# Row gathers in pairs and held-back scatters in layer 0 of a two-layer graph network, on one core

## The reference

```python
h = maximum(layernorm(x), 0)
msg = relu(h[src] + edge_attr_16 @ W_edge.T + b_edge)          # layer 0
agg = segment_sum(msg, dst, 6250)
x = x + (relu(batchnorm((h + agg) @ W1.T + b1)) @ W2.T + b2)
h = maximum(layernorm(x), 0)
Y = relu(concat(h[src], edge_attr_64) @ M_W.T + M_b)           # layer 1
Z = segment_sum(Y, dst, 6250)
x = x + relu(concat(h, Z) @ U_W.T + U_b)
```

## Time and profile before

| | us |
|---|---|
| Median of three runs (lowest, highest) | 4233.39 (4220.89, 4243.19) |
| Profiled execution, own time | 4231.45 |
| Span of the profiled execution | 4229.6 |
| Turns 2 to 29 of layer 0, those that the change touches | about 415 to 2947 of the span |
| Layer 1, paced turns and rest | about 3260 to 4180 of the span |
| Busy over the span: PE / PEld / DVE / ACT / POOL | 2624.5 / 2201.3 / 1525.2 / 965.0 / 2087.3 |

### The profile page before, as it was taken

One profiled execution on the slowest core, in us unless ns is written; L12 is line 12 of the kernel. 1 busy time (PEld: TensorE's weight loads), 2 busy tenths in 40 slices (PEclk: granted clock), 3 DMA queues, 4 the chain that ended last, 5 costly groups with the idle time before them and its releaser, 6 DMA issues.

```text
span 4229.6 us, 74366 instructions
## 1 busy us (share of the span) xinstructions
PE 2624.5 (62%) x25733; PEld 2201.3 (52%) x25733; DVE 1525.2 (36%) x2605; ACT 965.0 (23%) x2153; POOL 2087.3 (49%) x2185
## 2 busy tenths in 40 slices
PE   3456666566566556666656665656465767676665
PEld 3345555455455455555545555555454655555554
DVE  4323233223223323222323222323234555555553
ACT  1322222122222222222222222222134222222221
POOL 5444545544545544545454545544523455555554
PEclk9767666666666666667666667666676788878786
DMA  7545544545444544544454544544334666666661
GB/s 223 129 118 136 160 126 136 133 113 143 134 122 138 134 114 117 156 120 127 134 131 126 149 124 121 151 115 124 81 97 114 164 165 160 154 150 161 165 160 45
DMA packets 707917, 567.80 MB, mean 134 GB/s; under 512 B 495308, under 2 KB 609216, under 8 KB 703224
## 3 DMA queue, kind: packets, MB, share of 16 engines
q1 hardware_dynamic: 628632, 403.50, 37.8%
q0 software_dynamic: 69440, 107.94, 9.4%
q10 hardware_dynamic: 9632, 53.14, 3.4%
HBM read 296.20 MB, written 268.18 MB: 133 GB/s over the span
## 4 chain that ended last, share of the span: by engine, by line
PE 42%; issue 27%; another core or an unknown queue 17%; DVE 9%; ACT 3%; DVEq 1%; DMA 1%; ACTq 0%; SPq 0%; POOL 0%; POOLq 0%
PE ps_w L1223 19%; PE ps_p L1158 10%; PE ps_r L1211 7%; PE ps_b L1193 3%; DVE arena L1624 2%; PE ps_p L1150 2%; DVE ranking L1550 1%; DVE arena L1633 1%; DVE arena L1647 1%; ACT arena L921 1%; ACT plain_e L901 1%; ACT arena L934 1%; DVE arena L1609 0%; DMA src_store<-arena 0%
## 5 line engine op out<-in xcount | busy, mean ns | idle before, releaser
L748 POOL DMA_INDIRECT edge_store<-side,slot_idx x1054 | 1017.8, 966 | 1155.9 <-issue 707.4
L1223 PE MATMUL ps_w<-arena 128*64 128x128 f32 (+1 forms) x9040 | 1179.3, 324 | 584.1 <-issue 418.1
L778 POOL DMA_INDIRECT gathered_rows<-node_table_l,plain_slot x1116 | 1061.7, 951 | 890.5 <-issue 300.3
L1223 PEld LDWEIGHTS ps_w<-arena 128*64 128x64 f32 x9040 | 926.5, 174 | 743.6 <-issue 558.8
L1624 DVE TENSOR_TENSOR arena<-ps_c,dst_rel 128x1024 f32<-128x1024 f32 (+1 forms) x476 | 526.5, 1106 | 853.1 <-remote 449.8
L1158 PE MATMUL ps_p<-w_both,side 80*128 80x128 f32 x3228 | 638.9, 357 | 278.1 <-DVE ranking L1550 102.1
L934 ACT ACTIVATE arena<-arena 128x512 f32<-128x512 f32 (+1 forms) x616 | 366.3, 595 | 1710.0 <-remote 602.4
L1158 PEld LDWEIGHTS ps_p<-w_both,side 80*128 80x128 f32 x3228 | 556.1, 258 | 323.6 <-issue 251.8
L1609 DVE TENSOR_SCALAR arena<-arena,iota_p 125x512 bf16<-125x512 bf16 (+1 forms) x442 | 152.5, 354 | 1211.9 <-ACT arena L921 782.7
L921 ACT ACTIVATE arena<-ps_b 125x512 bf16<-125x512 f32 (+1 forms) x442 | 247.7, 576 | 865.6 <-remote 749.6
L1211 PE MATMUL ps_r<-tab,arena 125*128 125x64 bf16 x5100 | 305.7, 219 | 210.3 <-issue 138.5
(11 more groups left out here) (124 smaller groups left out, 1132.5 us busy)
## 6 DMA issues: line engine op xcount, KB each, us to landing
edge_store<-zeros SPq DMA_DIRECT2D x34, 3300.0 KB
arena<-edge_store SPq DMA_DIRECT2D x34, 1650.0 KB
src_store<-arena SPq DMA_DIRECT2D x204, 256.0 KB
side<-attr SPq DMA_DIRECT2D x172, 256.0 KB
arena<-edge_store SPq DMA_DIRECT2D x34, 1056.0 KB
arena<-edge_store SPq DMA_DIRECT2D x34, 594.0 KB
plain_store<-plain_e SPq DMA_DIRECT2D x35, 512.0 KB
side<-plain_store SPq DMA_DIRECT2D x35, 512.0 KB
```

What stands on the lines that cost most here:

```text
L748: pool.indirect_dma_start(out=store, in_=stage[:, c, i, :], in_offset=None, out_offset=bass.IndirectOffsetOnAxis(ap=slot_idx[:, s, t + i:t ...
L778: pool.indirect_dma_start(out=rows[s][:, i, :], out_offset=None, in_=table[layer], in_offset=bass.IndirectOffsetOnAxis(ap=plain_slot[:, s, ...
L1223: mm = pe.matmul(ps_sum[layer][t % 2][:, 0:width], msg[:, slot, t, :], dst_match[:, slot, t, 0:width], start=(first and t <= layer), stop= ...
```

## The change

`ROW_STEPS` goes. In layer 0 each pair of gathers now waits until a half unit of group m + 1 is spread: pairs 0 to 7 for half units 0, 1, 1, 2, 2, 3, 4 and 5. And in the paced scatters, the third transfer of each chunk but the last waits until the next chunk is staged. Nothing else differs; layer 1 is untouched.

```diff
-ROW_STEPS = (NK - 1, NK - 1, NK, NK)
+PAIR_HALVES = (0, 1, 1, 2, 2, 3, 4, 5)
 CHUNK_STEPS = (1, 1, 2, 2, 3, 4, 5, 6)
...
-            def scatter(m, s, c):
+            def scatter(m, s, c, paced):
+
                 t, nt = CHUNKS[c]
                 for i in range(nt):
+                    if paced and i == 2 and c + 1 < len(CHUNKS):
+                        pool.wait_ge(evacuated_n, evacuated(m, c + 1))
+                        pool.sem_inc(pool_released, 1)
                     pool.indirect_dma_start(
...
-                    scatter(m, s, c)
+                    scatter(m, s, c, paced)
...
                     for i in range(v * UNIT, v * UNIT + nt):
-                        if paced and layer == 0 and i % CHUNK == 0:
-                            pool.wait_ge(dense_sems[0].scattered, after_step(m - 1, ROW_STEPS[i // CHUNK]))
+                        if paced and layer == 0 and i % 2 == 0:
+                            pool.wait_ge(bcast_done, halves(m + 1, PAIR_HALVES[i // 2]))
                             pool.sem_inc(pool_released, 1)
```

## The result

The changed kernel takes 4130.37 us (median of four runs, 4116.80 to 4142.51), the kernel before 4234.16 us (four runs, 4220.89 to 4243.19). The ratio is 0.9747, with a 95% interval of 0.9705 to 0.9789: 2.5% faster, 104 us, where 42 us were forecast. The profiled execution took 4142.51 us, 88.9 us less than that of the kernel before.

A forecast was written before the change was run, and what follows sets the result against it. The prediction took freezes of the other engines during POOL's unbroken pieces of scatters and gathers as the bound. Its terms, -71 + 28 + 1 = -42 us against 4231.45 us, gave 4190 us, range 4075 to 4305 us (8 in 10).

The forecast's parts named there:

- the premise: In paced layer 0 turns, POOL's unbroken piece of scatters or gathers sets when a freeze ends, 2.7 or 3.3 us later.
- Freezes: Stretches where POOL works alone and other engines nearly stop; two a turn, over scatters of chunks 0 to 3 and gathers.
- Part 1: Scatters of chunks 0 to 3: POOL stops after 14, not 16, ending the freeze 2.5 us earlier a turn, -71 us.
- Part 2: After chunk 4's staging: held scatters lengthen POOL's next piece, costing about 5 us in one turn in five, +28 us.
- Part 3: Row gathers: they start earlier, moving the freeze from the prefix to the steps before it; nearly cancelling, +1 us.
- The twin: Unpaced turn 30, 16 gathers right behind chunk 7: 33.0 us to the prefix's end, less 5.0 us gave 28.0 us.
- The third freeze: Rival: another freeze between chunk 3's second pair and chunk 7, 5 us each, 4302 us if every turn; chance 0.28.
- Pauses that break the freezes: Rival: POOL stops after ten scatters every turn, 213 us won in place of 71, 4048 us; chance 0.13.
- The bound that the prediction put on such a pause: A pause in POOL's piece must be longer than about a microsecond and a half to count.
- the 1 us that the prediction names: Lower end of the 1 to 12 us it gave the prefix in turns whose gathers are split.
- Nothing moves: Rival: DMA load sets the turn, freezes ignore POOL's piece, or gains are given back; 4231 us within 15; chance 0.23.
- What would show it: Timeline signs: 14 scatters first, chunk 4 staged at 23.2 us, gathers right behind chunk 7, stopping at the 13th, prefix 1 to 6 us.

The follow-up runs named there:

- the scatters alone: Kernel before with only the third-scatter waits added, gathers keeping their old waits: 4252.55 us, ratio 1.0058; 2887.77 us where the kernel before took 2888.14 us.
- The gathers alone: Kernel before with only the paired gather waits, scatters keeping their old waits: 4134.85 us, ratio 0.9747; 2885.32 us where the kernel before took 2888.14 us.

## Why the prediction was right and wrong

**The direction and the premise** held. Freezes exist in the profiled kernel, an unbroken piece of POOL sets their end there, and splitting the gathers gained time. The size did not: 104 us for 42, and the term that was set to nothing brought all of it.

**Part 1 (first piece of 14).** The mechanism held for this stretch: 14 scatters in the usual turn, and chunk 4 staged 22.8 to 23.1 us after the first scatter in 25 of 28 turns, 23.2 us forecast. In the three others POOL paused after ten, and it took 17.5 to 18.3 us. The mean gain is 3.3 us a turn, -92 us, for the forecast -71.

**Part 2 (what follows).** Mis-sized: forecast +1.0 us a turn, measured +1.9 (+54 us) in the changed kernel and +3.8 (+105 us) with the scatters alone. Of the 1.9 us, 1.2 us are PE's "issue" idle (0.8 us before, 2.0 us in the changed kernel). The argument that a piece only 2 us longer than the time PE still runs costs little did not hold.

**Part 3 (gathers in pairs).** This is the step that failed. The prediction priced the stretch from the first half unit to the end of the prefix at 28.0 us, against 29.6 us in one-piece turns and 25.4 us in split ones, and got +1 us. Two things were wrong in it. First, the two rows were no means. Cut as the prediction cuts it, from the start of the first spreading, the stretch takes 32.6 us on average in the 17 one-piece turns (turn 12 is one of three short ones) and 24.8 in the 11 split ones; with these the same formula gives -43 us. The changed kernel takes 30.1 us, not 28.0, which gives +16 us. So +1 us lay near the measured value of this stretch by two misses that nearly cancel. Second, the stretch was cut at the wrong event. It ends where the next turn can start, at the next first scatter. In a split turn of the kernel before, the second eight gathers run behind the prefix and freeze the steps after it. Two windows of the kernel before show it, each from the end of the prefix to the next first scatter, a split turn and then a one-piece turn:

```profile
1300.88:1319.91 19.03, 11.71 (x89) 10.90 (x86) 8.84 (x21) 3.92 (x9) 7.38 (x9) 0.59 0.13 23
1395.32:1409.52 14.20, 11.82 (x88) 11.14 (x85) 7.14 (x11) 3.80 (x9) 0.00 (x0) 0.62 0.07 12
```

Nearly the same matmuls, 89 and 88, take 19.0 us beside POOL's second piece and 14.2 us without it. So to the next first scatter a one-piece turn takes 45.9 us and a split one 43.3 (means of 17 and 11), a mean of 44.9. In the changed kernel the gathers are done before the prefix ends: 29.6 + 13.3 = 43.0 us. That is -2.0 us a turn, -55 us, where the prediction had +1: the stretch up to the prefix is 0.7 us longer, the one behind it 2.7 us shorter. The gathers alone took 96 us off. The twin that it used, the unpaced turn 30, lacks the pause before the last four gathers, and I had put right only its length, not what the rest of the turn gets from it.

The sum with the measured terms: -92 + 54 - 55 = -93 us, against 89 us between the two profiled executions.

**What the terms did not show**, and only the experiments did: they are stretches of the turn, not edits, and what the held scatters win in the first they lose in the next two. With the gathers paired, holding the scatters changes nothing: 87.1 us a turn with and without (4134.85 us and ratio 0.9747 alone, 4130.37 us and 0.9747 together). The table's columns for the two say where it goes: 3.3 us won up to chunk 4, 2.0 lost up to the first half unit, 1.5 up to the prefix. From the first scatter to the end of the last gather it is 72.4 us in both. That POOL's queue, with the same 47 instructions, sets this length is my reading; no run isolates it. Holding the scatters alone leaves that stretch at 74.8 us, 75.1 before. So the 2.5% is the gathers', and the prediction had it from the scatters: right in sign for the wrong part.

**The rivals.** The third freeze came in part: 1.9 of the 5 us, 1.2 of them PE's "issue" idle, and with the scatters alone 3.8 us and a kernel that is slower. Pauses that break the freezes came in three turns of 28. The bound that the prediction put on such a pause is borne out by the turns of the kernel before: with a gap of 1.14 us behind eight gathers (turn 6) the prefix took 19.3 us, with gaps of 1.80 to 1.82 us 9.7 to 11.7. In the ten split turns with such a gap or a longer one it took 6 to 12 us; the 1 us that the prediction names is that of turn 29, whose gathers are those of the unpaced turn 30. "Nothing moves" is what happens where the kernel before takes 2888 us: there POOL's issue sets the turn. The rule of the Trainium skill (Trainium Kernel Development and Optimization, Key Constraints), that the DMAs of all queues share 16 engines and interleave, gives no account of the freezes: the largest queue, SP's, took 55.1% of 2885.0 us = 1590 us of those engines' time without them, and with them

```profile
span 4140.5 us, 74786 instructions
...
q1 hardware_dynamic: 628632, 403.50, 38.3%
```

38.3% of 4140.5 us = 1586 us. Its transfers cost the same with freezes and without.

**What would show it**: chunk 4's time and the prefix at 1 to 6 us were found (2.4 us from the seventh half unit to its end, on average). The gathers start 1.7 us behind chunk 7 on average, sooner than before but not right behind it, as they do with the gathers alone (0.3 us in most turns). The pause came before the 13th gather in most turns, before the 11th in the turn shown.

**Open** stays what makes the freezes come and go, and what resource they are. Not settled either is where between one DMA in 1.51 us and one in 1.74 us they end, and whether the mean over some microseconds is what counts or a backlog behind POOL that a rate above some 1.5 us drains. The latter would fit the freeze's outlasting a piece by 3 us, but no run shows such a queue. The kernels with the late zero fill and with the first piece of 12 ran only without freezes, so what part the fill's transfers have in the first freeze is untested; against them speaks only that PE stands still at a DMA share of 0.17 in the second.

## What to carry to other kernels

Close a stretch whose cost you compare at the event that lets the next round start, not at the step that looks freed, and compare whole rounds of each kind first: 92.6 against 87.0 us stood in the trace of the kernel before. A wait that only moves a queue's instructions within a round is worth nothing if the round goes by that queue's last one. And before tuning against a stall, see whether it is there in every session: here the same program had another bound some 40 minutes later, by the record's times, and while pauses behind every fourth DMA shortened the time by 7% in the one case, shorter ones lengthened it by 11 and 14% in the other.

## What the runs showed of the hardware

- The same kernel before took 4231 to 4289 us in four comparisons and 2887 to 2888 us in two, each steady within its comparison (2881.92 to 2892.57 us in 31 runs). The record names the same chip for one comparison of each kind. POOL's own speed is alike: one indirect DMA in 1.26 us in both. With freezes PE's matmuls come single and 0.7 us and more apart while POOL issues without a pause (6 in 8 us in the earlier trace rows), against 464 in a turn of 59.5 us without.
- With freezes, the progress of the other engines went by the mean rate of POOL's indirect DMAs: three piece lengths (4, 6, 8) at one in 1.5 us gave 4197, 4198 and 4193 us (beside 4289 us), one in 1.74 us gave 3937 us (beside 4231 us) although POOL then works almost throughout. PE's "issue" idle is 16 to 19 us a turn in the former and 3.6 us in the latter.
- A small memset on POOL that is waited for costs far more than its 0.23 us: 0.77 us a pause, where POOL is the bound.
